# Scan stage of a GNN and Mamba kernel: lower products, loads and hand-over by chunks of 512 rows, another order of the small steps, and accumulating transfers for pair adds

## What is computed

```python
h = relu(layernorm(x))
x = x + relu(((adj * d[:, None] * d[None, :]) @ h) @ W.T + b)   # d = (row sums of adj + 1e-9) ** -0.5

h = relu(layernorm(x))
h = relu(adj @ h @ gcn_w + gcn_b)
h = layernorm(h) * ln_g + ln_b
xz = h @ w_in;  xc, z = xz[:, :256], xz[:, 256:]
u = silu(causal_conv4(xc, conv_w) + conv_b)
dbc = u @ w_xp
dt = softplus(dbc[:, :8] @ w_dt + b_dt);  B = dbc[:, 8:24];  C = dbc[:, 24:]
for each row t:   state = exp(dt * A) * state + dt * B * u;   y[t] = state @ C     # 256 channels x 16 states
x = x + ((y + u * D_skip) * silu(z)) @ w_out
```

## Time and profile before

| what | value |
|---|---|
| median of 3 runs | 2634.03 us (2629.68 to 2637.1) |
| the profiled execution | 2630.88 us |
| its span, first to last instruction | 2629.1 us |
| mean granted clock of TensorE | 0.948 of full |
| TensorE, VectorE, ScalarE, GpSimd busy | 85%, 79%, 37%, 41% of the span |
| first product L677 of slot 0 | at 1480.4 us |
| HBM read, written | 625.28 MB, 16.25 MB |

### The profile page before, as it was taken

How to read it: one execution, slowest core, us unless ns; L and a number is a source line. 1 busy time by engine, 2 the same in 40 slices (tenths; PEclk the granted TensorE clock), 3 DMA queues, 4 the chain that set the end, 5 groups by cost and what they waited for, 6 DMA issues and landing times.

```text
span 2629.1 us, 21933 instructions
## 1 busy us (share of the span) xinstructions
PE 2242.3 (85%) x6864; PEld 1272.3 (48%) x6864; DVE 2075.4 (79%) x2079; ACT 978.3 (37%) x1696; POOL 1067.6 (41%) x461
## 2 busy tenths in 40 slices
PE   0347889999999999999999988888989888886776
PEld 0222444444448888888885434444434443443333
DVE  7889988887536666666653599999999999999997
ACT  0100000000015555554552455555545554555552
POOL 0000000000000000000000399999999999998554
PEclk9968889999999999999999999999999999997898
DMA  9999999889766665565547656565556565651221
GB/s 391 396 423 417 419 405 385 357 365 364 253 243 235 220 215 213 200 216 195 194 163 273 228 208 224 209 216 208 212 206 221 203 224 194 216 209 64 73 73 52
DMA packets 108323, 643.00 MB, mean 245 GB/s; under 512 B 14224, under 2 KB 15024, under 8 KB 42672
## 3 DMA queue, kind: packets, MB, share of 16 engines
q1 hardware_dynamic: 92160, 604.02, 60.6%
q10 hardware_dynamic: 16048, 37.57, 4.0%
HBM read 625.28 MB, written 16.25 MB: 244 GB/s over the span
## 4 chain that ended last, share of the span: by engine, by line
PE 54%; DVE 24%; DMA 9%; issue 8%; ACT 3%; DVEq 0%; SPq 0%; ACTq 0%
PE ps L841 21%; PE ps L759 14%; DMA ring<-adj 9%; PE ps L881 9%; DVE ps L677 7%; DVE arena L692 5%; DVE arena L584 4%; PE ps L959 3%; DVE ring L692 3%; PE ps L910 2%; PE ps L902 1%; DVE parts L718 1%; PE ps L963 1%; PE ps L921 1%; DVE arena L726 1%
## 5 line engine op out<-in xcount | busy, mean ns | idle before, releaser
L452 POOL TENSOR_TENSOR rstd<-base,minus_half 128x8 f32<-128x8 f32 (+1 forms) x40 | 84.7, 2117 | 1422.4 <-DVE base L504 813.2
L841 PE MATMUL ps<-adj_parts,h_parts 128*128 128x512 f32 x2592 | 593.4, 390 | 2.9 <-ACT adj_parts L1055 1.9
L881 PE MATMUL ps<-ring,diag_h 128*128 128x512 f32 x1152 | 562.1, 623 | 0.9 <-DVE arena L664 0.9
L584 DVE TENSOR_TENSOR arena<-arena,ring 128x2048 f32<-128x2048 f32 x208 | 476.9, 2293 | 90.8 <-DMA ring<-adj 79.1
L841 PEld LDWEIGHTS ps<-adj_parts,h_parts 128*128 128x128 f32 x2592 | 484.7, 188 | 109.1 <-ACT adj_parts L1055 5.0
L759 PE MATMUL ps<-ring,arena 128*128 128x512 f32 x928 | 433.4, 627 | 59.0 <-DMA ring<-adj 58.9
L692 DVE TENSOR_TENSOR_SCAN arena<-arena,state,ps 128x512 f32<-128x512 f32 x312 | 382.4, 1267 | 29.5 <-ACT arena L1130 9.7
L468 POOL TENSOR_TENSOR arena<-arena 128x1024 f32<-128x1024 f32 x156 | 377.5, 2431 | 67.7 <-ACT state L1122 67.6
L881 PEld LDWEIGHTS ps<-ring,diag_h 128*128 128x128 f32 x1152 | 228.0, 200 | 251.7 <-issue 246.8
L601 DVE TENSOR_TENSOR adj_parts<-ring,adj_parts 128x1024 fp32r<-128x1024 f32 x216 | 264.0, 1224 | 94.7 <-ACT adj_parts L1055 84.1
L1130 ACT ACTIVATE arena<-arena,a_sb 128x512 f32<-128x512 f32 x512 | 338.3, 708 | 0.4
(11 more groups left out here) (93 smaller groups left out, 1970.2 us busy)
## 6 DMA issues: line engine op xcount, KB each, us to landing
ring<-adj SPq DMA_DIRECT2D x480, 1024.0 KB, 6.7
arena<-c_scratch SPq DMA_DIRECT2D x128, 512.0 KB, 4.1
diag_h<-adj SPq DMA_DIRECT2D x32, 1024.0 KB, 12.4
arena<-x ACTq DMA_DIRECT2D x16, 512.0 KB, 6.0
x_scratch<-arena ACTq DMA_DIRECT2D x8, 512.0 KB, 3.0
arena<-x_scratch ACTq DMA_DIRECT2D x16, 256.0 KB, 5.0
out<-arena ACTq DMA_DIRECT2D x16, 256.0 KB, 3.8
lower_scratch<-arena ACTq DMA_DIRECT2D x7, 512.0 KB, 2.9
```

Of the source, the lines that this page charges most:

```text
L584: nc.vector.tensor_tensor(acc, acc, v, ALU.add).then_inc(adds_done, 1)
L841: last = nc.tensor.matmul(acc[:, c, :], h_parts[:, blk % 2, layer, h_part, a * F:(a + 1) * F], adj_parts[:, buf, adj_part, c * MM:(c + 1) ...
L881: last = nc.tensor.matmul((acc_c if i else y_ps)[:, c, :], tile_of(h1, JT * s + a), blk[:, a * STRIP + c * MM:a * STRIP + (c + 1) * MM], s ...
```

## The change

- **By chunks.** A load of pass C brings, for one chunk of 512 target rows, four groups of 128 source rows (two halves of blocks) in one transfer of 1 MB. For this the columns inside a block are laid out with the chunk outermost; passes A and B read them through other access patterns. The products are counted in units (chunk, load, group). Chunks 0 and 1 use the banks of `y_ps`, later ones the two banks of `acc_c` in turn, and the first product of chunk k waits for the hand-over of chunk k-2. There are 15 adds of 128x512 and a copy for 7 adds and a copy of 128x1024, and three buffers `s1` of 512 columns.
- **Products over slots.** 24 units ahead of slot -24, one in each slot up to -5, then evenly up to slot 215. The hand-overs come to -24, -16, -8, -2, 8, 18, 31, 44, 61, 78, 97, 117, 140, 164, 190 and 216.
- **Slots of the small steps** as in the constants below. Modulo 16: GCN goes from 13 to 8, BIAS from 13 to 9, STATS and POWER from 15 to 11, NORMALISE from 1 to 13, OUT from 9 to 14, RESIDUAL from 9 to 15, the store from 9 to 0, LOAD_X1 from 12 to 6.
- **From VectorE to GpSimd**: w (slot 15 to 14) and the gate.
- **Exponentials** two slots ahead, in three buffers.
- **Pair adds.** For the first three quads of a chunk GpSimd issues one accumulating transfer that adds the second pair of slots to the first (1 MB, SBUF to SBUF) and, three slots later, adds the two remaining slots itself. The last quad has its three adds as before. PE sums the first three quads two slots later (QSUM 9 for 7).
- **Rows of C** in three buffers, loaded one pair earlier.

```diff
-GCN, BIAS, STATS, POWER, NORMALISE = -19, -19, -17, -17, -15
+GCN, BIAS, STATS, POWER, NORMALISE = -24, -23, -21, -21, -19
 TRANSPOSE, XZ, SILU, DBC, SPLIT = -13, -12, -7, -6, -5
-DT, SOFTPLUS, WEIGHTED_U = -4, -3, -1
-QSUM, NSUM = 7, 6
-LOAD_X1, SKIP, GATE, OUT, RESIDUAL = 12, 20, 21, 25, 25
+DT, SOFTPLUS, WEIGHTED_U = -4, -3, -2
+QSUM, NSUM = (9, 9, 9, 7), 6
+LOAD_X1, SKIP, GATE, OUT, RESIDUAL, STORE = 22, 20, 21, 30, 31, 32
...
+    for g in range(FIRST_SLOT, end):
+        due += 1 if g < DT else (len(rest) - n - due) / (end - g)
+        while due >= 1 - 1e-6 and n < len(rest):
+            k, p, j = rest[n]
+            last = (p, j) == (pairs_of[k][-1], PJ - 1)
+            if k > 3 and g < handover.get(k - 2, end) or last and g + 1 < DS * (k - S1B) + GCN + 3:
+                break
+            products[g].append(rest[n])
+            n, due = n + 1, due - 1
+            if last:
+                handover[k] = g + 1
...
-        da = [work2(HALVES, T) for _ in range(2)]
+        da = [work2(HALVES, T) for _ in range(3)]
...
+                if loads[q][0] == "C":
+                    strip, c = divmod(i, CPS)
+                    rows_in = adj[2 * s:2 * s + 2, strip, :, c * JT * T:(c + 1) * JT * T]
+                    sp.dma_start(ring[:, slot_of[q], :].rearrange("p (s a) -> p s a", s=2),
+                                 rows_in.rearrange("s p a -> p s a")).then_inc(ring_in[slot_of[q]], 16)
...
             for g in slots:
-                pair = (g + 2) // 2
+                pair = (g + 4) // 2
...
-                    if pair >= 2:
-                        sp.wait_ge(mult_done, 2 * pair - 2)
+                    if pair >= CSB:
+                        sp.wait_ge(mult_done, 2 * (pair - CSB) + 2)
...
+                k = chunk_at(g, WEIGHTED_U)
+                if k is not None:
+                    if k >= 2:
+                        pool.wait_ge(dbu_done, DS * (k - 1))
+                    pool.wait_ge(dt_ready, k + 1)
+                    pool.wait_ge(u_ready, k + 1)
+                    nc.gpsimd.tensor_tensor(w[k % 2], dt[k % 2], u[k % 2], ALU.mult).then_inc(w_ready, 1)
+                k = chunk_at(g, GATE)
+                if k is not None:
+                    pool.wait_ge(y_free, k + 1)
+                    pool.wait_ge(sz_ready, k + 1)
+                    nc.gpsimd.tensor_tensor(yg, yg, sz[k % 2], ALU.mult).then_inc(yg_ready, 1)
...
                     nc.gpsimd.tensor_tensor(buf, buf, c_row, ALU.mult).then_inc(mult_done, 1)
-                    if g % 2 and g < QUAD_CHUNKS * DS:
+                    k, n = divmod(g, DS)
+                    if k < QUAD_CHUNKS and n % 4 == 2 and n >= 6:
+                        q = g // 4 - 1
+                        pool.wait_ge(quad_in, 16 * (q - k + 1))
+                        first, second = (hs[(4 * q + j) % HSB] for j in range(2))
+                        nc.gpsimd.tensor_tensor(first, first, second, ALU.add).then_inc(quad_done, 1)
+                    if k < QUAD_CHUNKS and n % 4 == 3 and n < DS - 4:
+                        pool.wait_ge(mult_done, g + 1)
+                        pool.dma_start(hs_pairs[(g // 2 - 1) % (HSB // 2)], hs_pairs[g // 2 % (HSB // 2)],
+                                       accum_op=ALU.add).then_inc(quad_in, 16)
+                    if k < QUAD_CHUNKS and n % 2 and n >= DS - 4:
                         pool.wait_ge(mult_done, g + 1)
                         even = hs[(g - 1) % HSB]
                         nc.gpsimd.tensor_tensor(even, even, buf, ALU.add).then_inc(pair_done, 1)
...
-                        nc.vector.tensor_tensor(halves(s1[i % 2]), acc_c if i else y_ps, halves(s1[i % 2]), ALU.add)\
-                            .then_inc(s1_ready, 1)
+                        nc.vector.tensor_tensor(s1[k % S1B], sums_in, s1[k % S1B], ALU.add).then_inc(s1_ready, 1)
...
-                if 0 <= g + 1 < NCH * DS:
-                    k, n = divmod(g + 1, DS)
+                if 0 <= g + 2 < NCH * DS:
+                    k, n = divmod(g + 2, DS)
...
-        "adj": np.asarray(adj).reshape(NS, STRIP, NB, JT, P).transpose(2, 0, 4, 3, 1).reshape(NB, NS, P, BLOCK),
+        "adj": np.asarray(adj).reshape(NS, CPS, T, NB, JT, P).transpose(3, 0, 5, 1, 4, 2).reshape(NB, NS, P, BLOCK),
```

More of the change, by code:

```diff
@@ L144, in build @@
             blocks_at[q] = blocks
[L148 removed]
+    FIRST_SLOT, LAST_SLOT = GCN, DS * (NCH - 1) + STORE + 1
     slots = list(range(FIRST_SLOT - 1, LAST_SLOT))
     products = {g: [] for g in slots}
[L151 to L154 removed]
+    units = {k: [(k, p, j) for p in pairs_of[k] for j in range(PJ)] for k in range(NCH)}
+    ahead = BPS // 2 * PJ
+    products[FIRST_SLOT - 1] = units[2][:ahead] + units[3][:ahead] + units[0]
+    rest = units[1] + units[2][ahead:] + units[3][ahead:] + [unit for k in range(4, NCH) for unit in units[k]]
     handover = {0: FIRST_SLOT}
[L158 to L168 removed]
+    end = DS * (NCH - 1) + GCN
+    n, due = 0, 0.0
+    for g in range(FIRST_SLOT, end):
[9 more added lines that the diff above has]
+                handover[k] = g + 1
+                assert g + 1 <= DS * k + GCN
+    assert n == len(rest)
+    block_end = {load_at["C", k, p]: g for g in slots for k, p, _ in products[g]}
     misc = []
@@ L226, in work2 @@
             return v
-        s1 = [work2(STRIP) for _ in range(2)]
+        s1 = [work2(T) for _ in range(S1B)]
         gbuf = work2(CT, F)
@@ L241, in build @@
               for b in range(HSB)]
-        csb = [work2(2, T) for _ in range(2)]
+        csb = [work2(2, T) for _ in range(CSB)]
         yg = work2(HALVES, T)
@@ L310, in build @@
         l1_out = sem("l1_out")
-        l1_back = [sem(f"l1_back{i}") for i in range(2)]
+        l1_back = [sem(f"l1_back{i}") for i in range(S1B)]
         l0_out = [sem(f"l0_out{i}") for i in range(2)]
@@ L332, in build @@
         c_out = sem("c_out")
-        c_in = [sem(f"c_in{i}") for i in range(2)]
+        c_in = [sem(f"c_in{i}") for i in range(CSB)]
         da_ready = sem("da_ready")
@@ L780, in fold @@
                     for a in range(JT):
-                        last = nc.tensor.matmul(ps_deg[:, t:t + 1],
-                                                rowacc[i % 2][:, a * STRIP + t * P:a * STRIP + (t + 1) * P], ones[:, :],
+                        col = (t // CT * JT + a) * MM + t % CT * P
+                        last = nc.tensor.matmul(ps_deg[:, t:t + 1], rowacc[i % 2][:, col:col + P], ones[:, :],
                                                 start=a == 0, stop=a == JT - 1)
```

153 lines of the change are left out of this document (69 added, 84 removed).

## The result

The changed kernel takes **2653.91 us** (median of 4 runs, 2647.88 to 2660.87), the kernel before 2633.92 beside it: ratio 1.0079, 95% interval 1.0058 to 1.0101. The forecast was 2622, faster. The time is inside the range (2596 to 2662), but on the other side of no change. The profiled execution took 2649.65 us, with a span of 2647.5 against 2629.1.

A forecast was written before the change was run, and what follows sets the result against it. TensorE was taken to bound the lead-in, VectorE's chain of scans the chunks, GpSimd close behind. Savings (-17, -18.3, -23.4, -32) and costs (+0.7, +52.2, +22, +3, +0.8) summed to -12.0: 2622 us beside the median, range 2596 to 2662.

The forecast's parts named there:

- lead-in: Up to the first scan, TensorE sets the time; fewer lower products ahead of slot 0 were to save 17 us.
- w and gate off VectorE: Scan stage: fifteen w and fifteen gate instructions leave VectorE for GpSimd, -18.3 and -23.4 us.
- waits for exponentials: Scan stage: the scans' 14.8 us of waiting for ScalarE go, with exponentials two slots ahead in three buffers.
- waits of L677 (L723) for B rows: Scan stage: 17.2 us of waits for TensorE go with the bias moved; new TensorE waits cost 22.
- hand-over: Scan stage: twelve smaller adds for six, +0.7 us, TensorE no longer waiting; lower products meeting chunk 13's sums, +3.
- w late: End of each chunk: w ready at T+11.9, needed at T+8.1 (T: nmr written, behind scan 13); +52.2 us.
- accumulating transfers: Three 1 MB transfers a chunk, issued by GpSimd, land before they are needed, at least 11.2 us later: 0 us.
- last gate, tail: The last gate stands in the tail, not hidden on GpSimd: 2.4 us for 1.56, +0.8.
- The prediction's own signs: Right: lead-in near 64 us, fifteenth slot longest. Wrong: chunk mean above 71.6 without late transfer, meaning TensorE's waits underpriced.
- rival A: Chunk's end: w is in time, 52 us more gained, about 45 let through by GpSimd and TensorE: 2577; chance 15%.
- Rival B: Slots 6, 10 and 14: accumulating transfers land after 12 us, GpSimd waits; up to 39 us per microsecond, 2662; chance 22%.
- Rival C: Shared SBUF port: VectorE's work lengthens w on GpSimd, one microsecond more each, +13 us, 2635; chance 13%.

## Why the prediction was wrong

Forecast and measurement by the prediction's steps, in us. The measured column is from the two traces; where it says nothing else, it is for chunks 0 to 12, after less before.

| step | forecast | measured |
|---|---|---|
| lead-in | -17 | -18.0, and 0.6 ahead of it |
| w and gate off VectorE | -41.7 in the scan stage | -34.9 here (15.8 and 19.1 before, 0 after) |
| waits for exponentials | -14.8 | -12.9, all of them in this stretch |
| waits of L677 (L723) for B rows | -17.2 + 22 | 17.2 before, 19.7 after: +2.5, most before slot 7 |
| hand-over | +0.7, and +3 at its end | adds +0.4, **VectorE's waits before them +12.0** |
| w late | +52.2 | +44.2; 49.3 in 15 times over the whole trace |
| accumulating transfers | 0 | landing 10.6 to 12.5; 0 by the run without them |
| **statistics and split in one slot** | **no term** | **+21.7 in L550 and L764** |
| residual's wait for TensorE | no term | -2.4 |
| last gate, tail | +0.8 | +2.2 |

The measured terms of chunks 0 to 12 add up to 30.6; the other 4.3 of the 34.9 us are waits under 1 us, and gaps and overlaps between records.

**The step that failed** is the slots of the small steps. The prediction follows NORMALISE to slot 13, for its effect on w, and the bias to slot 9, but it has no term for STATS and POWER going from slot 15 to 11. It let these small instructions move at nothing, without a reason. Two things were to be asked. What covered them where they stood? In the kernel before slot 15 is the longest at 7.82; in the changed one a wait of 3.8 us was forecast for just this slot by the prediction itself, so the statistics taken out of it could not shorten it. And what do they meet in their new place? The split with two inputs in SBUF, beside GpSimd's products. Undoing the move gave 53 us: slot 11 shrank by 3.5 us a chunk, slot 15 by 0.7, slots 13 and 6 by 0.3 each, while slot 1 grew by 0.5. The version without the move wins 31 us, more than the 12 forecast. How the 53 us divide between the statistics and the normalisation was not tried by one run each. The run that moved only the normalisation, on top of another order of GpSimd, gave 22.

The prediction's own signs say the same. It named slot 15 as the longest of a chunk, and it is slot 11. A chunk mean above 71.6 with no late transfer, it said, would mean that TensorE's waits were underpriced; the mean is 74.24, and of what the sum lacked 21.7 us are the split and the added constant, 12.0 the hand-over.

**TensorE's waits** are right in size for L723, 21.0 us for the 22 forecast, but by luck. The mechanism forecast was an idle TensorE: the u product behind ScalarE's ReLU, some 3 us. That wait is there, 1.6 us in the mean:

```profile
PE ps L1007 <- ACT arena L1213: 19.1, 12, 3.1
```

but no product of VectorE in the slot behind it waited for a B row. 17.0 of the 21.0 us stand before slot 7, where TensorE is full. With the gate gone, slots 5 and 6 together are only 0.25 us a chunk shorter, not 1.56: the prediction booked the gate's whole time as won and did not ask what TensorE does in those slots.

**The hand-over** was mis-sized: +0.7 for the adds is right, but their own waits for the last lower product were put at nothing, and took 17.9 us over the trace (10.4 and 7.5), 12.0 of them in chunks 0 to 12; before there were none in this stage. The prediction had only asked whether TensorE waits for the adds.

**The late w** was right in place, cause and size: w was ready 12.4 us behind the scan of slot 13 in the mean, beside T+11.9 forecast. Right, too, that it is not simply to be had back: but rival A's price was wrong. It said that with w in time 45 us would come through; w in time gave 0 (2653.95 us), because the same GpSimd queue is waited for again in slot 2, then in slot 4. The prediction went by the engines' sums (GpSimd 9 us less a chunk) and not by the order in which its queue serves VectorE.

**Rival B** fell: the transfers landed in 10.6 to 12.5 us (page, DMA issues, median), at the far bound of the earlier trace rows and beyond the 11.2 available, and yet GpSimd (L509) waited for them 8 times, 13.9 us in all (6.6, 4.7 and 2.6 by buffer): for most of the 39 it came late itself.

```profile
arena<-arena POOLq DMA_DIRECT2D x16, 1024.0 KB, 11.7
...
arena<-ring POOLq DMA_DIRECT2D x8, 1024.0 KB, 12.5
ring<-ring POOLq DMA_DIRECT2D x8, 1024.0 KB, 10.6
```

The estimate of 4.4 us by the Trainium skill, DMA: Bandwidth & Descriptors, section Anatomy of one DMA, is not near these; the measurement decides.

**Rival C** named the right resource and the wrong place. It priced the port for w on GpSimd, which kept its 2.35 us throughout; it was VectorE's small instructions in slot 11 that were lengthened. The prediction had the row for it, L740 beside the lengthened product, but looked for GpSimd as the one to pay.

One reading of the rows was off as well: the prediction calls GpSimd close behind VectorE, but in the earlier trace rows it is ahead, busy for 68.9 of 70.9 us against 66.1. That VectorE paced the chunk all the same is shown by the split from PSUM on the kernel before: chunks 0 to 12 fell from 71.56 to 70.75 us in the mean, with nothing taken off GpSimd.

## What to carry to other kernels

Price a moved instruction twice: by what covered it where it stood, and by what runs beside it where it goes; an instruction that fills a wait is free, and the same one four slots earlier was not. Do the same with an instruction that is taken away: ask which engine will need the time that it covered. Where one engine's queue feeds another in several places, taking away the largest wait can give nothing until the queue itself starts earlier: follow the queue, not the wait. When a change of many parts disappoints, look for the part that has no term in the sum and undo that one alone.

## What the hardware did that was not expected

- A VectorE instruction on 128x4 numbers took 0.17 us alone and up to 2.27 beside a GpSimd instruction of 2.35, and the profile books it as busy time, with no idle time before it. One with two inputs in SBUF (40x512) took 2.79 for 0.69, and 128x1024 took 3.33 for 1.2. Where the split started first, the GpSimd instruction took 2.69 and 2.78 instead. So the minimum, median and maximum of one line show such a conflict, while the list of waits does not.
- The blocked time moves: with L550 gone, the split and L554 took 20 of its 23 us over (15 x 0.27 and 14 x 1.17).
- Accumulating transfers of 1 MB from SBUF to SBUF, 39 of them beside the loads, raised the DMA engines' share of this stage from 0.6 to 0.8 and lengthened the loads of adj from 6.8 us (the run without them) to 8.5 in the median, with no difference in the kernel's time.
